# Windowed attention with a gate: high halves of q on ScalarE's queue, row maxima placed by ScalarE

## The reference

```python
xn = layernorm(x)
q, k, v = xn @ Wq + bq, xn @ Wk + bk, xn @ Wv + bv      # 32 query heads, 8 key/value heads, 64 wide
q, k = rope(q) * SCALE, rope(k) * SCALE                 # pairs of even and odd elements turned
scores = q @ k.T, or -1e9 where |row - column| > 128    # 4 query heads share a key head
probs = softmax([scores, sink of the head])             # the sink's column is dropped after it
s = (probs @ v) @ Wo + bo
g = silu(fp8_rounded(xn) @ weight.T + bias)
out = x + s * g
```

## Time and profile before

| | |
|---|---|
| three runs | 2068.41, 2087.06 (median) and 2089.49 us |
| profiled execution | 2074.46 us, its span from first to last instruction 2072.7 us |
| mean granted TensorE clock | 0.907 |
| busy: PE, PEld | 1807.7 us (87%), 1592.2 us (77%) |
| busy: DVE, POOL, ACT | 1277.2 us (62%), 1011.2 us (49%), 730.8 us (35%) |
| transfers | 151.95 MB, 39.8% of the time of 16 DMA engines |

### The profile page before, as it was taken

How to read it: one execution, slowest core, us unless ns; L and a number is a source line. 1 busy time by engine, 2 the same in 40 slices (tenths; PEclk the granted TensorE clock), 3 DMA queues, 4 the chain that set the end, 5 groups by cost and what they waited for, 6 DMA issues and landing times.

```text
span 2072.7 us, 34158 instructions
## 1 busy us (share of the span) xinstructions
PE 1807.7 (87%) x11139; PEld 1592.2 (77%) x11139; DVE 1277.2 (62%) x4157; ACT 730.8 (35%) x1509; POOL 1011.2 (49%) x1019
## 2 busy tenths in 40 slices
PE   2498999989899889898889989898999988899888
PEld 1287878877788777787778878887788877788777
DVE  7755665655656557556566665665666666565564
ACT  2133333333333433333333333343343333333332
POOL 3345444554444644545544553554455465445441
PEclk8579899989998899889999999998999999999899
DMA  4634334344254343443344343344335434442530
GB/s 145 129 68 69 65 63 83 72 78 74 37 94 70 67 78 51 81 75 67 68 78 80 57 88 65 59 92 84 60 53 95 80 64 71 77 66 54 95 65 17
DMA packets 81728, 151.95 MB, mean 73 GB/s; under 512 B 13712, under 2 KB 30864, under 8 KB 77456
## 3 DMA queue, kind: packets, MB, share of 16 engines
q1 hardware_dynamic: 81552, 149.76, 39.8%
HBM read 18.64 MB, written 4.19 MB: 11 GB/s over the span
## 4 chain that ended last, share of the span: by engine, by line
PE 68%; issue 6%; DVE 6%; SPq 5%; ACT 4%; DMA 4%; POOL 3%; POOLq 0%; DVEq 0%
PE pv_bank L1132 23%; PE ring L1093 10%; PE acc L1155 8%; PE ring L1044 8%; PE score L1116 7%; PE score L1118 6%; PE ring L1142 3%; SPq L364 3%; ACT stage L619 2%; PE ring L1053 2%; DMA qT_full<-q_second_hi 2%; DMA kT_low<-k_second 2%; POOL k_first L520 1%; POOL k_second L522 1%; SPq L366 1%
## 5 line engine op out<-in xcount | busy, mean ns | idle before, releaser
L854 DVE CUSTOM_DVE_ANT_0 junk<-ring,mask 128x384 bf16<-128x384 f32 (+1 forms) x1024 | 497.3, 488 | 646.1 <-PE ring L1093 636.2
L1132 PEld LDWEIGHTS pv_bank<-v,stage 128*128 128x128 f32 x5120 | 708.3, 206 | 14.4 <-issue 5.8
L1132 PE MATMUL pv_bank<-v,stage 128*128 128x65 f32 x5120 | 713.8, 282 | 0.6 <-DVE o_norm L886 0.4
L542 POOL TENSOR_SCALAR_AFFINE_SELECT stage<-stage 128x512 f32<-128x512 f32 x384 | 246.8, 656 | 833.9 <-ACT stage L619 833.7
L1093 PE MATMUL ring<-kT_high,qT_full 128*128 128x384 f32 (+1 forms) x1024 | 411.6, 403 | 165.9 <-DMA kT_low<-k_second 71.0
L619 ACT ACTIVATE stage<-score 128x512 f32<-128x512 f32 x640 | 357.5, 597 | 335.5 <-PE score L1118 334.0
L1093 PEld LDWEIGHTS ring<-kT_high,qT_full 128*128 128x128 f32 x1024 | 213.2, 208 | 209.0 <-issue 129.7
L1116 PE MATMUL score<-qT_full,kT_high 128*128 128x512 f32 x640 | 279.0, 436 | 16.1 <-ACT stage L619 14.1
L660 ACT ACTIVATE oT_hi<-ring 128x256 fp32r<-128x256 f32 x256 | 98.6, 385 | 518.5 <-PE ring L1142 518.5
L1118 PE MATMUL score<-qT_high,kT_low 72*128 72x512 f32 x640 | 267.8, 418 | 0.0
L1116 PEld LDWEIGHTS score<-qT_full,kT_high 128*128 128x128 f32 x640 | 132.2, 207 | 68.9 <-ACT stage L619 48.7
(11 more groups left out here) (119 smaller groups left out, 2651.9 us busy)
## 6 DMA issues: line engine op xcount, KB each, us to landing
qT_high<-qT_full SPq DMA_DIRECT2D x64, 512.0 KB, 4.5
qT_full<-q_first SPq DMA_DIRECT2D x64, 256.0 KB, 4.2
qT_full<-q_first_hi SPq DMA_DIRECT2D x64, 256.0 KB, 5.6
qT_full<-q_second SPq DMA_DIRECT2D x64, 256.0 KB, 6.9
qT_full<-q_second_hi SPq DMA_DIRECT2D x64, 256.0 KB, 8.0
kT_high<-k_first_hi SPq DMA_DIRECT2D x128, 64.0 KB, 3.3
kT_high<-k_second_hi SPq DMA_DIRECT2D x128, 64.0 KB, 3.1
qT_high<-turned_rows SPq DMA_DIRECT2D x512, 2.0 KB
```

The source lines that it names most:

```text
L542: nc.gpsimd.affine_select(out=pr, in_=pr, compare_op=ALU.is_ge, fill=0.0, base=0, pattern=[[0, GROUP], [sign, P]], channel_multiplier=-sign) \
L854: nc.vector.tensor_tensor_reduce(junk[:, h % 2, 0:cols], ring[h % 2][:, 0:cols], mask[:, m0:m0 + cols], 1.0, LOWEST, ALU.add, ALU.max, row ...
L1132: last = nc.tensor.matmul(pv[:, h, :], prob[:, q % 2 * 3 + n, h * P:(h + 1) * P], v[:, slot, k, :], start=(n == 0), stop=(n == len(BLOCKS[ ...
```

## The change

It has two parts. The two high transfers of a step are issued by ScalarE (`highs_placed`) in slot q == 3 of the same step, behind the copy of the turned output and ahead of the keys' high parts, under the same waits; SyncE's `lows_in` keeps the two low ones. And the row maxima no longer go through `turned_rows`: ScalarE writes the 8x256 block four times, once for each head, straight into the 8 partitions of `qT_high`, with a factor per partition from `own_rows`, which is 1 in the two rows of the head and 0 in the others. So the zeros are written with them, VectorE's memset of `qT_high` at the start goes, and GpSimd makes `own_rows` there with a memset and two selects. The score matmuls wait for ScalarE's copies in place of the transfers.

```diff
--- before.py
+++ after.py
@@ -203,7 +203,7 @@
         kT_low = sb("kT_low", [P, 3, SEQ], F32R)
         v = sb("v", [P, V_SLOTS, TILES, DV], F32)
         neg_parts = sb("neg_parts", [P, 2, 2, NR], F32R)
-        turned_rows = sb("turned_rows", [NR, 2 * P], F32)
+        own_rows = sb("own_rows", [NR, GROUP], F32)
         junk = sb("junk", [P, 2, 3 * P], BF16)
         row_max = sb("row_max", [P, 2, 2, GROUP], F32)
         neg_max = sb("neg_max", [P, 2, GROUP], F32)
...
@@ -365,17 +365,14 @@
                 for row, part in ((0, k_first), (HALF, k_second)):
                     sp.dma_start(kT_low[row:row + HALF, t % 3, :].bitcast(F32), part[r, :]).then_inc(s_kT_in, 16)
 
-            def queries_in(a):
-
-                parts = ((0, q_first, q_first_hi, s_first_lo, s_qT_first_in),
-                         (HALF, q_second, q_second_hi, s_second_lo, s_qT_second_in))
+            def lows_in(a):
+
                 upto(sp, s_score_pe, NB * (a - 1))
-                for row, low, high, ready, done in parts:
+                for row, low, ready, done in ((0, q_first, s_first_lo, s_qT_first_in),
+                                              (HALF, q_second, s_second_lo, s_qT_second_in)):
                     sp.wait_ge(ready, a + 1)
                     upto(sp, done, Q_IN * a)
                     sp.dma_start(qT_full[row:row + HALF, a % 2, :, :].bitcast(F32), low[:, :]).then_inc(done, 16)
-                    sp.dma_start(qT_full[D + row:D + row + HALF, a % 2, :, :].bitcast(F32), high[:, :]) \
-                        .then_inc(done, 16)
 
             def highs_in(b):
 
...
@@ -384,15 +381,6 @@
                 upto(sp, s_qT_high_in, 16 * b)
                 sp.dma_start(qT_high[0:D, b % 2, :, :].bitcast(F32), qT_full[D:2 * D, b % 2, :, :].bitcast(F32)) \
                     .then_inc(s_qT_high_in, 16)
-
-            def rows_in(s, pair):
-
-                sp.wait_ge(s_max_rows_done, 2 * s + pair + 1)
-                if s == 0 and pair == 0:
-                    sp.wait_ge(s_ones_ready, 3)
-                for h in range(GROUP):
-                    sp.dma_start(qT_high[D + 2 * h:D + 2 * h + 2, s % 2, h, pair * 2 * P:(pair + 1) * 2 * P]
-                                 .bitcast(F32), turned_rows[2 * h:2 * h + 2, :]).then_inc(s_rows_in, 16)
 
             def result(n, j):
 
...
@@ -406,14 +394,10 @@
                     highs_in(b)
                 if real(t) and t % QUAD:
                     keys_in(t)
-                if real(it):
-                    rows_in(it, 1)
                 if k == 0 and n >= 1:
                     result(n - 1, 0)
-                if real(it + 1):
-                    rows_in(it + 1, 0)
                 if real(a):
-                    queries_in(a)
+                    lows_in(a)
                 if real(t) and t % QUAD == 0:
                     keys_in(t)
                 if k == 0 and n >= 1:
...
@@ -459,9 +443,16 @@
             nc.gpsimd.memset(minus_half[:, :], -0.5).then_inc(s_id_memset, 1)
             nc.gpsimd.memset(v[:, :, :, :], 1.0).then_inc(s_id_memset, 1)
             nc.gpsimd.memset(ones[:, :], 1.0).then_inc(s_ones_ready, 1)
-            pool.wait_ge(s_id_memset, 5)
+            nc.gpsimd.memset(own_rows[:, :], 1.0).then_inc(s_id_memset, 1)
+            pool.wait_ge(s_id_memset, 6)
             nc.gpsimd.affine_select(out=ident[:, :], in_=ident[:, :], compare_op=ALU.not_equal, fill=1.0, base=0,
                                     pattern=[[-1, P]], channel_multiplier=1).then_inc(s_id_ready, 1)
+
+            nc.gpsimd.affine_select(out=own_rows[:, :], in_=own_rows[:, :], compare_op=ALU.is_ge, fill=0.0, base=0,
+                                    pattern=[[-2, GROUP]], channel_multiplier=1).then_inc(s_rows_self, 1)
+            pool.wait_ge(s_rows_self, 1)
+            nc.gpsimd.affine_select(out=own_rows[:, :], in_=own_rows[:, :], compare_op=ALU.is_ge, fill=0.0, base=1,
+                                    pattern=[[2, GROUP]], channel_multiplier=-1).then_inc(s_id_ready, 1)
 
             nc.gpsimd.affine_select(out=mask[:, 0:P], in_=mask[:, 0:P], compare_op=ALU.is_ge, fill=MASKED, base=0,
                                     pattern=[[1, P]], channel_multiplier=-1).then_inc(s_id_ready, 1)
...
@@ -640,6 +631,16 @@
                 nc.scalar.activation(q_second_hi[:, :].bitcast(F32R), q_second[:, :], ACT.Copy) \
                     .then_inc(s_second_hi, 1)
 
+            def highs_placed(a):
+
+                upto(act, s_score_pe, NB * (a - 1))
+                for row, high, ready, done in ((D, q_first_hi, s_first_hi, s_qT_first_in),
+                                               (D + HALF, q_second_hi, s_second_hi, s_qT_second_in)):
+                    act.wait_ge(ready, a + 1)
+                    upto(act, done, Q_IN * a)
+                    nc.scalar.dma_start(qT_full[row:row + HALF, a % 2, :, :].bitcast(F32), high[:, :]) \
+                        .then_inc(done, 16)
+
             def keys_high(quad):
                 act.wait_ge(s_k_summed, 2 * quad + 2)
                 nc.scalar.activation(k_first_hi[:, :].bitcast(F32R), k_first[:, :], ACT.Copy).then_inc(s_k_hi, 1)
...
@@ -648,9 +649,10 @@
             def max_rows(s, pair):
 
                 act.wait_ge(s_max_turned_pe, 2 * s + pair + 1)
-                upto(act, s_rows_in, 16 * GROUP * (2 * s + pair))
-                nc.scalar.activation(turned_rows[:, :].bitcast(F32R), ring[2][0:NR, 0:2 * P], ACT.Copy) \
-                    .then_inc(s_max_rows_done, 1)
+                for h in range(GROUP):
+                    last = nc.scalar.activation(qT_high[D:D + NR, s % 2, h, pair * 2 * P:(pair + 1) * 2 * P],
+                                                ring[2][0:NR, 0:2 * P], ACT.Copy, scale=own_rows[:, h:h + 1])
+                last.then_inc(s_max_rows_done, 1)
 
                 nc.scalar.activation(sink_exp[:, s % 2, 2 * pair:2 * pair + 2, :], sink_arg[:, pair, :, :], ACT.Exp) \
                     .then_inc(s_sink_done, 1)
...
@@ -693,6 +695,8 @@
                     if q == 1 and real(a):
                         first_high(a)
                         second_high(a)
+                    if q == 3 and real(a):
+                        highs_placed(a)
                     if q == 3 and k in (2, 6) and quad < BATCH * QUADS:
                         keys_high(quad)
                     if it < 0 and fill + FIRST_CHUNKS < N_CHUNKS:
...
@@ -1111,7 +1114,7 @@
                 if n == 0 and q == 0:
                     pe.wait_ge(s_qT_high_in, 16 * (c + 1))
                 if n == 0 and q % 2 == 0:
-                    pe.wait_ge(s_rows_in, 16 * GROUP * (2 * c + q // 2 + 1))
+                    pe.wait_ge(s_max_rows_done, 2 * c + q // 2 + 1)
                 upto(pe, s_exp_done, NB * c + blk - 1)
                 nc.tensor.matmul(score[blk % 2][:, :], kT_high[:, c % 3, k * P:(k + 1) * P],
                                  qT_full[:, c % 2, :, q * P:(q + 1) * P], start=True, stop=False)
```

9 lines of the change are left out of this document (4 added, 5 removed).

## The result

The changed kernel takes 2170.23 us (median of 4 executions, 2165.03 to 2180.47); the kernel before took 2087.28 (4 executions, 2068.41 to 2089.49). The ratio is 1.0426, with a 95% interval of 1.0364 to 1.0487: slower. The profiled execution took 2165.03 us with a span of 2163.3, against 2074.46 and 2072.7: 90.6 us more.

The account below looks back on a forecast made before the run. TensorE's instruction stream was taken as the bound, the last query transfer ending last at many step heads. 19.9 - 4.8 + 3 + 19.5 + 17.6 + 19.5 = 75 us over 2074.46 gave 2149, forecast as 2150, range 2090 to 2205.

Parts of the forecast that it names:

- the terms 19.9, -4.8, 3, 19.5 and 17.6: Microseconds for late highs, gain at it % 8 == 3 and 4, it % 8 == 1, key steps, and held turns.
- The issue behind the oT_hi copy: Highs issued after that copy's end in slot q == 3 delay heads at it % 8 == 5, 7, 0: 19.9 us.
- The kind it % 8 == 7: Steps whose last high lands 10.9 us after SyncE's first issue, against 10.0 before: 0.9 us lost in each of 7.
- The gain in the kinds 3 and 4: Sixteen steps with it % 8 == 3 or 4 gain 0.3 us each from earlier landing: -4.8 us.
- The kind it % 8 == 1: Steps with a projection between: 3 us lost over 8 steps, bounds 0 and 10.
- The keys: In 15 key steps two issues ahead of the k_first_hi copy start its chain 1.3 us later: 19.5 us.
- The copies: Four copies hold TensorE's turn of the output at q == 0 by 0.55 us in 32 steps: 17.6 us.
- The clock: Lower granted clock after longer waits at the heads of 23 steps, 0.85 us each: 19.5 us, bounds 0 and 78.
- The first (2215 us): Everything near its upper end, copies 52 us, clock 39, no gain at it % 8 == 3 and 4; chance 0.13.
- The second: ScalarE's issues cost nothing, copies follow at 0.28 us, clock holds: 25 us more, 2099 us; chance 0.15.
- the third: High transfers move beside the low ones, each landing 4.2 us after its issue: faster, 2017 us; chance 0.12.
- the fourth: Two queues hinder each other, the high pair needs 8.2 us instead of 6.2: 2240 us; chance 0.04.

Follow-up runs that it names:

- experiment 3: The changed kernel with ScalarE issuing the high transfers right behind the second exp of slot q == 3, ahead of its waits: 1.0262 of the kernel before.
- Experiment 4: The changed kernel with the keys' high copies ahead of the high query issues in ScalarE's order in key steps: 1.0433 of the kernel before.
- experiment 11: The kernel before with the four copies alone, plus one further scratch copy that TensorE's turns must wait for (0.36 us longer hold): 1.0497.
- experiment 12: The kernel before with the four copies alone, plus three further scratch copies that TensorE's turns must wait for (1.08 us longer hold): 1.1135.
- experiment 2: The kernel before with only the high transfers moved to ScalarE behind the oT_hi copy, row maxima still by small transfers: 1.0293.
- experiment 9: The changed kernel with the row maxima first copied out of the bank to SBUF and the four copies made from there: 1.0293 of the kernel before.
- experiment 1: The kernel before with only the four ScalarE copies of the row maxima, all query transfers still on SyncE: 1.0246.
- experiment 10: The changed kernel with the four copies made from SBUF and the high transfers issued right after the second exp of slot q == 3: 1.0177.
- experiment 5: The kernel before with the four copies alone, made from SBUF behind one copy that empties the bank and frees TensorE: 1.0046.
- experiment 6: The kernel before with only head 0's copy of the row maxima, heads 1 to 3 left out, for timing alone: 1.0020.
- experiment 8: The kernel before with only the high transfers moved to ScalarE, issued right after the second exp of slot q == 3: 1.0028.
- experiment 7: The kernel before, row transfers kept, with three further scratch copies from the bank that TensorE's turns must wait for: 1.0107.

## Why the prediction was right

The forecast was 2150 us, 3% above the median of before, and the range reached from 2090 to 2205; 2170.23 lies inside, 20 us above the forecast, and the direction and the mechanism were those given. Point by point, against the profiled execution (75 us forecast, 90.6 measured):

- **Without the clock** the terms 19.9, -4.8, 3, 19.5 and 17.6 make 55.2 us; measured were 52.0 us of idle time, 36.1 at the heads (37.6 forecast), 13.0 at the turns (17.6), 5.8 at the turning of maxima (none forecast). That the heads' sum agrees within 2 us is partly luck: 6.0 of the 36.1 us are waits for row_max that no term has, the gain of 4.8 didn't come, and the terms for keys, late heads and it % 8 == 1 were each too large.
- **The issue behind the oT_hi copy.** I counted from the copy's end; the first high is issued 0.08 us after its start (1102.43 and 1102.51), 0.3 us earlier. Its landing follows as said. At it % 8 == 5 the head comes 10.99 us after the first issue for 10.33 before and waits 0.50 us, a loss of 0.7 where 1.3 was forecast; at 0 it waits 1.09 where 0.76 + 0.4 was.
- **The kind it % 8 == 7** loses more, 1.92 us of idle where 0.18 + 0.9 was forecast. SyncE's load of x (1135.95) stood behind four query transfers before and now stands ahead of ScalarE's two. The trace shows that it is the load: in the six such steps that have one the next head waits 1.69 to 1.92 us, in the last (1920.45), which has no x left to load, 0.64. That is the kind of neighbour that a moved issue passes, and I hadn't looked for it.
- **The gain in the kinds 3 and 4** didn't come. A head of such a step waited 1.88 us (1.79 before in the earlier trace rows); the highs queue behind the lows, as experiment 3 shows in isolation.
- **The kind it % 8 == 1**: its next head waits for nothing in either trace (1211.58 here), where 3 us were forecast.
- **The keys**: 15.0 us more in 16 waits, 19.5 forecast. The k_first_hi copy starts 1.34 us after the start of the oT_hi copy (1102.43 and 1103.77) and started 0.28 us after it before (1071.34 and 1071.62), so the two issues cost 1.06 us and not 1.3. Experiment 4 took it away by order alone.
- **The copies**: the spacing is 1.08 / 3 = 0.36 us, as estimated; held were 13.0 us in 35 waits, 17.6 in 32 forecast.
- **The clock is the term that was too small**: 19.5 us forecast, 38.6 measured in TensorE's busy time, within the bounds of 0 to 78. I charged it to the 23 steps whose head waits longer, with the held turns as an aside. A good part does lie behind such heads: the six that follow a load of x had 1.00 in the next 8 us before and have 0.79, 0.60, 0.58 and three times 0.57 now, which makes 8 x 2.32 = 18.6 us (an estimate from the windows' granted clocks), at fewer steps than I charged and more for each. The longer waits for the keys could cost little clock, since the stretch behind them was slow before too. But the held turns cost clock as well, about one for each us by experiments 11 and 12, and for them the sum has no term. How the 38.6 us divide between the two isn't shown: experiments 2 and 9, with the heads' waits and no hold, have 17 and 13 us of the rest, experiment 1, with the holds alone, 31, each within 13 to 15.
- **Rivals.** The first (2215 us) was right that the clock's term is about 39 and that the kinds 3 and 4 gain nothing, and wrong that the copies hold TensorE for 52 us (13.0). The second (no cost for issues and copies) fell with experiments 1, 2 and 4; the third with experiment 3; the fourth too, since the landings stay 2 us apart with two queues.

**What stays open** is how much clock a short hold in the middle of dense work costs against a longer wait at a head, and why. Nor do these runs settle how much of it is the chip's: experiment 10 has 22 ± 16 us of the rest with hardly a hold, while experiments 5, 6 and 8, on a chip where the kernel before already ran at 0.904, have 5, -2 and -8. No variant was run on two chips, so the two can't be told apart.

No variant beats the kernel before. The removed row transfers were worth nothing (experiment 6: 1.0020), as their 1.8 us of waits had said.

## What to carry to other kernels

Before moving a transfer to another engine's queue, write down when that engine reaches the issue and everything that it passes on both queues: here the second queue gave no bandwidth, the place behind a late copy cost some 20 us of idle time, the place ahead of a critical copy 15, and even the early place 8 to 10 us ahead of the xqT copies. A PSUM bank that another engine waits for should be emptied by one short copy and the work be done from SBUF: four copies from the bank held TensorE for 13 us and their staged form not at all. Where the clock falls after pauses, short holds of the bounding engine inside dense work should not be charged at their length alone; here they cost about double (experiments 11 and 12, one kernel on one chip).

## What the hardware showed that I hadn't expected

- A transfer issue on ScalarE starts 0.08 us after the start of the copy ahead of it in program order, and not after its end (1102.43, 0.38 us long, and 1102.51); but the copy behind two issues waits for them (1103.77).
- ScalarE's copy of 8x256 out of PSUM takes 373 ns without and 451 ns with a factor per partition, and 494 ns with the factor out of SBUF (experiments 5 and 7 for the first, the changed kernel, experiment 5). The copies follow one another every 0.28 (as the earlier trace rows show for the first) and 0.36 us.
- The kernel before ran at a mean granted clock of 0.910, 0.904 and 0.913 on three chips: whatever is to be compared within 2% has to be run in one call on one chip.
